# Shared experts in one stage, and expert rows added to the output by an adding scatter DMA

## The chip, the core and the metric

One NeuronCore of a Trainium2 chip runs the whole program in one launch. The metric is the device time of a run in microseconds, the median of several runs. The engines are PE (TensorE), DVE (VectorE), ACT (ScalarE), POOL (GpSimd) and SP (SyncE, which here only issues DMAs). They run side by side and are ordered by semaphores alone.

## The reference

Sixteen sequences of 512 tokens, width 256, all float32. A layer-normed attention block with 16 heads comes first, then a mixture-of-experts block. What matters here is the second half:

```python
x = x + attention(layernorm(x))                # called x1 below
xf = layernorm(x)                              # 8192 rows of 256
w  = top-2 of softmax(layernorm(xf) @ gate_w.T), normalised
out = swiglu(xf, sWg, sWu, sWd)                # the shared expert, every row
for e in range(8):                             # 256 -> 512 -> 256 each
    out = out + w[:, e:e+1] * swiglu(xf, Wg[e], Wu[e], Wd[e])
x = x + out
```

## The kernel before, in words

The attention stage and a short route stage come first and are not touched but for one table. The route stage gives each token two places in a list `xs_d` of 135 slots of 128 rows, sorted by expert; a slot belongs to one expert. `place` holds, for each token and choice, the row where the result goes and its weight. Then come three stages, each a block that all engines leave together.

**Scatter stage** (`scatter_stage`). ACT writes each tile of 128 normed rows into a ring buffer (L1460, L1462), and POOL scatters it twice into `xs_d` with an indirect DMA (L1491): 64 tiles, 128 scatters. Beside this the stage runs the shared expert (`SharedExpert`) for the first 11 of the 16 sequences. Its work is cut in rounds, one per sequence: PE does gate and up products (L1067) in four parts, the transposes of the next sequence (L1054), and after the second part the down products of the sequence before (L1081); ACT does the silu (L1116) and after each of the four parts writes some tiles' rows, `A_ROUND = (1, 2, 1, 2)` of them; DVE adds x1 to the result (`ysb`, L1183), and SP stores it to `ys_d`. All rounds are unrolled and each engine's order is written out by hand.

**Expert stage** (`expert_stage`). A loop over the 135 slots, software-pipelined over three slots. POOL loads a slot's rows (`xr`, L1594) two slots ahead and, two slots behind, scatters the slot's weighted result `y_e` (L1733) with an indirect DMA to `y2_d` (L1599). The destination `to` is the row in `y2_d` that belongs to the token and its choice; unused rows of a slot go to a spare row of their own. On each slot POOL issues the load first and then waits for `y_e`:

```python
pool.dma_start(xr[:, s.par], rows_of(xs_v, s.plus(2)))...
d = s.plus(-2)
pool.wait_ge(y_taken, d.v + 1)
nc.gpsimd.indirect_dma_start(y2_d[:, :], ...to[:, d.quad]..., y[:, d.par], None)
    .then_inc(y_stored[d.par], 16)
```

**Combine stage** (`combine_stage`). It loads the shared expert's weights again, runs the shared expert for the last five sequences, and adds the two expert results of each token to the shared result: on POOL for the first 11 sequences, on DVE for its own five. It reads `ys_d` and `y2_d` and writes the output.

Of the kernel before, what the change touches and what calls it, by code (L numbers as in the profile page):

```python
# [30 lines left out]
P = 128  # L31
# [22 lines left out]
SHARED_FIRST = 11  # L54
# [80 lines left out]
def build(nc, x, wqT, bq, wkT, bk, wvT, bv, woT, bo, J, lam, lns, lnb, gwT, Wg, Wu, Wd, sWg, sWu, sWd, out):  # L135
# [6 lines left out]
    ys_d = nc.dram_tensor("ys_d", [NT, P, D], F32, kind="Internal").ap()  # L142
    xs_d = nc.dram_tensor("xs_d", [NSLOT * P, XW], F32, kind="Internal").ap()
    y2_d = nc.dram_tensor("y2_d", [(NSLOT + 2 * NT) * P, D], F32, kind="Internal").ap()

    top = ExitStack()
    with top:
# [16 lines left out]
        with ExitStack() as c:  # L164
            moe_stages(nc, c, sbt, gws, gwb, lgT, Wg, Wu, Wd, sWg, sWu, sWd, out,
                       x1_d, ys_d, xs_d, y2_d, whi_d, wlo_d, ident, ones, mv2, eps)
# [756 lines left out]
def moe_stages(nc, ctx, sbt, gws, gwb, lgT, Wg, Wu, Wd, sWg, sWu, sWd, out,  # L923
               x1_d, ys_d, xs_d, y2_d, whi_d, wlo_d, ident, ones, mv2, eps):
    pos = sbt(ctx, "pos", [P, NT, 2], I32)
    slot_e = sbt(ctx, "slot_e", [1, NSLOT], I32)
    rstd2 = sbt(ctx, "rstd2", [P, NT])
    nmr = sbt(ctx, "nmr", [P, NT])
    place = sbt(ctx, "place", [P, NT, 2, 2])
    shared_weights = (sWg, sWu, sWd)  # L930

    with ExitStack() as c:
        with nc.cleanup_on_exit(), ExitStack() as c1:
            route_stage(nc, c1, sbt, ident, ones, mv2, eps, rstd2, nmr, place, lgT, gws, gwb, pos, slot_e)
        with ExitStack() as c1:
            scatter_stage(nc, c1, sbt, shared_weights, x1_d, ys_d, xs_d, ident, mv2, rstd2, nmr, place, pos)
    with ExitStack() as c:
        expert_stage(nc, c, sbt, whi_d, wlo_d, xs_d, y2_d, ident, slot_e)
    with ExitStack() as c:
        combine_stage(nc, c, sbt, shared_weights, x1_d, y2_d, ys_d, out, ident, mv2, rstd2)  # L940


class SharedExpert:
# [3 lines left out]
    def __init__(self, nc, ctx, sbt, tag, base, count, weights, x1_d, ys_d, ident, mv2, rstd2):  # L947
# [7 lines left out]
        self.x1_d, self.ys_d, self.ident, self.mv2, self.rstd2 = x1_d, ys_d, ident, mv2, rstd2  # L955
# [35 lines left out]
        self.a_store = 32 if base == 0 else 16  # L991
# [31 lines left out]
    def store(self, eng, s):  # L1023
        if not self.has(s):
            return
        ys_v = self.ys_d.rearrange("(c t) p d -> c p t d", t=TT)
        for j in range(2):
            eng.wait_ge(self.y_taken, s.v * 2 + j + 1)
            eng.nop(nofuse=True)
            eng.dma_start(self.batch_of(ys_v, s)[:, 2 * j:2 * j + 2], self.ysb[:, s.par, j]).then_inc(self.y_stored[s.par], 16)  # L1030
# [145 lines left out]
    def outputs(self, dve, s):  # L1176
        dve.wait_ge(self.x1_loaded[s.par], (s.half() + 1) * 16)
        for j in range(2):
            dve.wait_ge(self.y_ready, s.v * 2 + j + 1)
            if s.at_least(2) and j == 0:  # L1180
                dve.wait_ge(self.y_stored[s.par], s.half() * self.a_store)
# [18 lines left out]
def route_stage(nc, ctx, sbt, ident, ones, mv2, eps, rstd2, nmr, place, lgT, gws, gwb, pos, slot_e):  # L1200
# [76 lines left out]
    def _(pool):  # L1277
# [7 lines left out]
        nc.gpsimd.iota(place[:, :, :, 0].rearrange("p (b t) r -> p b t r", t=TT), pattern=[[S, NB], [1, TT], [NT * P, 2]], base=NSLOT * P,  # L1285
                       channel_multiplier=TT, allow_small_or_imprecise_dtypes=True).then_inc(iotas, 1)
# [100 lines left out]
def scatter_stage(nc, ctx, sbt, shared_weights, x1_d, ys_d, xs_d, ident, mv2, rstd2, nmr, place, pos):  # L1387

    FIRST, RING, AHEAD = SHARED_FIRST, 8, 3
    A_ROUND = (1, 2, 1, 2)  # L1390
# [6 lines left out]
    se = SharedExpert(nc, ctx, sbt, "_1", 0, FIRST, shared_weights, x1_d, ys_d, ident, mv2, rstd2)  # L1397
# [99 lines left out]
def expert_stage(nc, ctx, sbt, whi_d, wlo_d, xs_d, y2_d, ident, slot_e):  # L1497
# [15 lines left out]
    spare = sb("spare", [P, NSLOT])  # L1513
# [19 lines left out]
    spare_ready = sem("spare_ready")  # L1533
# [19 lines left out]
    xs_v = xs_d.rearrange("(s p) d -> s p d", p=P)  # L1553
    def over_slots(eng, step):
# [24 lines left out]
    def _(pool):  # L1579
        for r in range(2):  # L1580
            pool.dma_start(xr[:, r], xs_v[r]).then_inc(x_loaded[r], 16)
        nc.gpsimd.iota(spare[:], pattern=[[P, NSLOT]], base=0, channel_multiplier=1,
                       allow_small_or_imprecise_dtypes=True).then_inc(spare_ready, 1)

        def step(s):
# [9 lines left out]
            if exists(s.plus(-2)):  # L1595
# [3 lines left out]
                nc.gpsimd.indirect_dma_start(y2_d[:, :], bass.IndirectOffsetOnAxis(ap=to[:, d.quad], axis=0), y[:, d.par], None)\  # L1599
# [111 lines left out]
    def _(dve):  # L1711
# [33 lines left out]
        def destination(s):  # L1745
# [7 lines left out]
        dve.wait_ge(spare_ready, 1)  # L1753
# [3 lines left out]


def combine_stage(nc, ctx, sbt, shared_weights, x1_d, y2_d, ys_d, out, ident, mv2, rstd2):


    def sem(name):
        return ctx.enter_context(nc.semaphore(name))

    BASE, OWN = SHARED_FIRST, NB - SHARED_FIRST
    RING = 3
    acc = sbt(ctx, "acc", [P, RING, TT, D])
    yr = sbt(ctx, "yr", [P, RING, 2, TT, D])
    yo = sbt(ctx, "yo", [P, 2, 2, TT, D])
    loaded = [sem(f"loaded{r}") for r in range(RING)]  # L1770
    stored = [sem(f"stored{r}") for r in range(RING)]
    own_loaded = [sem(f"own_loaded{r}") for r in range(2)]
    final_done = sem("final_done")
    own_done = sem("own_done")
    se = SharedExpert(nc, ctx, sbt, "_2", BASE, OWN, shared_weights, x1_d, ys_d, ident, mv2, rstd2)
    block = ctx.enter_context(nc.Block())
    ys_v = ys_d.rearrange("(b t) p d -> b p t d", t=TT)
    y2_v = y2_d[NSLOT * P:, :].rearrange("(r b p t) d -> b p r t d", r=2, b=NB, p=P)
    out_v = out.rearrange("b (t p) d -> b p t d", p=P)

    @block.sync
    def _(sp):
        def load_rows(b):

            r = b % RING
            if b >= RING:
                sp.wait_ge(final_done, (b - RING + 1) * 2)
            sp.dma_start(yr[:, r], y2_v[b]).then_inc(loaded[r], 16)
            if b >= RING:
                sp.wait_ge(stored[r], b // RING * 16)  # L1790
            sp.dma_start(acc[:, r], ys_v[b]).then_inc(loaded[r], 16)

        def store(b):

            sp.wait_ge(final_done, (b + 1) * 2)
            sp.dma_start(out_v[b], acc[:, b % RING]).then_inc(stored[b % RING], 16)

        def load_own(o):

            if o >= 2:  # L1800
                sp.wait_ge(own_done, (o - 1) * 2)
            sp.dma_start(yo[:, o % 2], y2_v[BASE + o]).then_inc(own_loaded[o % 2], 16)

        def store_own(o):

            sp.wait_ge(own_done, (o + 1) * 2)
            sp.dma_start(out_v[BASE + o], se.ysb[:, o % 2].rearrange("p j t d -> p (j t) d")).then_inc(se.y_stored[o % 2], 16)

        se.load_in(sp, Batch(0, 0))
        se.load_weights(sp)  # L1810
        se.load_in(sp, Batch(0, 1))
        se.load(sp, Batch(0, 0))
        load_rows(0)
        se.load(sp, Batch(0, 1))
        se.load_in(sp, Batch(0, 2))
        load_rows(1)
        load_own(0)
        for b in range(2, RING):
            load_rows(b)
        load_own(1)  # L1820

        held = 0
        for s in range(OWN + 1):
            if s >= 1:
                se.load_in(sp, Batch(0, s + 2))
            for _ in range(2 if s < OWN else BASE - held):
                store(held)
                if held + RING < BASE:
                    load_rows(held + RING)
                held += 1  # L1830
            if s >= 1:
                store_own(s - 1)
                se.load(sp, Batch(0, s + 1))
                if s + 1 < OWN:
                    load_own(s + 1)
        for r in range(RING):
            sp.wait_ge(stored[r], (BASE - r + RING - 1) // RING * 16)
        for r in range(2):
            sp.wait_ge(se.y_stored[r], (OWN + 1 - r) // 2 * 16)

    @block.gpsimd
    def _(pool):
        for b in range(BASE):
            r = b % RING
            pool.wait_ge(loaded[r], (b // RING + 1) * 32)
            nc.gpsimd.tensor_tensor(acc[:, r], acc[:, r], yr[:, r, 0], ALU.add).then_inc(final_done, 1)
            pool.wait_ge(final_done, b * 2 + 1)
            nc.gpsimd.tensor_tensor(acc[:, r], acc[:, r], yr[:, r, 1], ALU.add).then_inc(final_done, 1)

    @block.tensor  # L1850
    def _(pe):
        se.transposes(pe, Batch(0, 0))
        pe.wait_ge(se.w_lo, 3)
        for s in range(OWN + 1):
            se.tensor_round(pe, Batch(0, s))

    @block.scalar
    def _(act):
        se.split_weights_hi(act)
        se.copies(act, Batch(0, 0))  # L1860
        for s in range(OWN + 1):
            se.scalar_round(act, Batch(0, s), lambda s, i: None)

    @block.vector
    def _(dve):
        def own_final(o):

            dve.wait_ge(own_loaded[o % 2], (o // 2 + 1) * 16)
            dve.wait_ge(se.y_taken, o * 2 + 2)
# [44 lines left out]
```

## Time and profile before

| | us |
|---|---|
| median of 3 runs (lowest to highest) | 2273.76 (2270.4 to 2279.28) |
| the profiled execution | 2278.09 |
| its span, first to last instruction | 2276.5 |
| scatter stage (1224.2 to 1478.4 of the span) | 254.2 |
| expert stage (1478.4 to 2151.4) | 673.0 |
| combine stage (2151.4 to 2276.5) | 125.1 |

The profile gives, for one execution, each instruction's start and length, what ended the idle time of its engine before it (the releaser), and the DMA traffic. The profiled execution's own time is 1.6 us more than its span and 4.3 us above the median of the runs. An arrow `<-` between tiles reads "written from"; after a wait it names the releaser; "issue" is a wait for nothing that the profile shows, and "remote" one whose releaser it could not name. The trace calls `y2_d` `y_d`. PE's ends are modelled.

### The profile page before, as it was taken

Reading aid. Unit: us, or ns where it says so; the run is one execution under the profiler, and the core shown is the slowest. Engines: PE = TensorE matmul, PEld = TensorE weight load, DVE = VectorE, ACT = ScalarE, POOL = GpSimd, SP = SyncE. Lnnn points to the kernel's source line nnn. Section 1 sums busy time; section 2 is a strip of 40 time slices with the busy share of each in tenths; the row PEclk is TensorE's granted clock in tenths of the full one; section 3 lists DMA queues with packets and bytes.
Section 4 is the critical chain, followed back from the end, with each engine's and each line's share of the span. In section 5 each row is a group of like instructions: output and inputs, shape, how many; then the busy total and the mean of one; then the engine's idle time right before and its main releaser. Section 6 shows DMA issues by size and latency. Waiting matters only on the chain. (4 is left out here: it accounts for less than half of the span.)

```text
span 2276.5 us, 47620 instructions
## 1 busy us (share of the span) xinstructions
PE 1993.5 (88%) x14698; PEld 1308.5 (57%) x14767; DVE 1289.2 (57%) x3898; ACT 1085.5 (48%) x2357; POOL 757.6 (33%) x1173
## 2 busy tenths in 40 slices
PE   2789999999999999999863988789999999999687
PEld 1344444545444454444432877667777777777576
DVE  5556666776666677666636443334554544455376
ACT  1155555555555555555422444345555555555331
POOL 1033333333333333333310555423333333333263
PEclk8599999999999999999975999989999999999899
DMA  7033344434334443433213555473111111111297
GB/s 211 29 112 110 114 132 133 123 117 126 110 114 132 133 125 115 126 110 105 89 63 111 179 185 178 145 297 133 56 56 57 57 57 55 57 55 57 101 330 270
DMA packets 156032, 276.87 MB, mean 122 GB/s; under 512 B 28576, under 2 KB 85152, under 8 KB 154848
## 3 DMA queue, kind: packets, MB, share of 16 engines
q1 hardware_dynamic: 133312, 219.13, 29.9%
q0 software_dynamic: 19104, 54.35, 7.1%
q8 instruction: 91, 1.49, 0.3%
q10 hardware_dynamic: 3456, 1.34, 0.2%
q14 instruction: 69, 0.57, 0.1%
HBM read 136.01 MB, written 96.26 MB: 102 GB/s over the span
## 5 line engine op out<-in xcount | busy, mean ns | idle before, releaser
L633 DVE CUSTOM_DVE_ANT_0 ps_rows<-ps_rows,maskrow 128x512 f32<-128x512 f32 (+3 forms) x1024 | 484.5, 515 | 304.3 <-PE ps_rows L490 303.4
L578 ACT ACTIVATE probs<-ps_cols 128x512 f32<-128x512 f32 (+3 forms) x1024 | 392.1, 435 | 387.7 <-PE ps_cols L501 381.1
L490 PE MATMUL ps_rows<-ks,qs 32*128 32x512 f32 (+3 forms) x2048 | 427.2, 492 | 85.7 <-DVE mx L633 48.7
L497 PE MATMUL ps_cols<-qs,ks 32*128 32x512 f32 (+3 forms) x2048 | 418.7, 485 | 2.5 <-ACT probs L578 2.4
L490 PEld LDWEIGHTS ps_rows<-ks,qs 32*128 32x128 f32 x2048 | 161.6, 188 | 294.9 <-DVE mx L633 245.6
L752 POOL TENSOR_TENSOR pace<-eps 1x1 f32<-1x1 f32 x256 | 58.4, 228 | 777.8 <-ACT probs L578 777.8
L501 PE MATMUL ps_cols<-mT,ones_r 32*128 32x512 f32 (+3 forms) x1024 | 285.3, 550 | 0.0
L1599 POOL DMA_INDIRECT y_d<-y_e,to x135 | 136.4, 1010 | 335.1 <-DVE y_e L1733 321.2
L1725 DVE TENSOR_TENSOR h_lo<-ps_h,h_hi 128x512 fp32r<-128x512 f32 x135 | 93.4, 692 | 229.5 <-ACT h_hi L1700 229.5
L1694 ACT ACTIVATE sg_e<-ps_ge 128x512 f32<-128x512 f32 x135 | 80.9, 599 | 264.2 <-PE ps_ge L1620 264.2
L514 PE MATMUL ps_o<-probs,vt 128*32 128x512 f32 (+3 forms) x2048 | 192.7, 448 | 0.8 <-POOL probs L754 0.8
L1491 POOL DMA_INDIRECT xs_d<-row,pos x128 | 128.5, 1004 | 155.4 <-ACT row L1462 123.4
L754 POOL TENSOR_SCALAR_AFFINE_SELECT probs<-probs 128x512 f32<-128x512 f32 x256 | 160.6, 627 | 0.0
L497 PEld LDWEIGHTS ps_cols<-qs,ks 32*128 32x128 f32 x2048 | 154.5, 184 | 9.3 <-ACT probs L578 7.6
L633 DVE DVE_READ_ACCUMULATOR2_ANT mx<- 128x1 f32 x1024 | 145.0, 142 | 0.1
L1067 PE MATMUL ps_g<-x2T,swg 128*128 128x512 f32 x384 | 107.2, 416 | 31.8 <-ACT sg L1116 15.4
L1741 DVE TENSOR_TENSOR h_e<-sg_e,ps_ue 128x512 f32<-128x512 f32 x135 | 92.9, 688 | 72.5 <-PE ps_ue L1620 72.5
L501 PEld LDWEIGHTS ps_cols<-mT,ones_r 32*128 32x128 f32 x1024 | 99.4, 188 | 51.5 <-issue 31.9
L1594 POOL DMA_DIRECT2D xr<-xs_d x133 | 73.7, 554 | 120.0 <-DVE to L1751 111.3
L1081 PE MATMUL ps_y<-swd,hT 128*128 128x256 f32 x768 | 100.8, 292 | 11.8 <-DVE hT L1164 8.3
L1620 PE MATMUL ps_ge<-w_hi,x_lo 128*128 x270 | 110.9, 492 | 0.0
L1620 PE MATMUL ps_ue<-w_hi,x_lo 128*128 x270 | 110.4, 490 | 0.0
(212 smaller groups left out, 3847.3 us busy)
## 6 DMA issues: line engine op xcount, KB each, us to landing
xs_d<-zrows SPq DMA_DIRECT2D x45, 408.0 KB, 2.9
xr<-xs_d POOLq DMA_DIRECT2D x135, 136.0 KB
whi_d<-w_sh SPq DMA_DIRECT2D x16, 768.0 KB, 3.8
w_hi<-whi_d SPq DMA_DIRECT2D x8, 1536.0 KB
yr<-y_d SPq DMA_DIRECT2D x11, 1024.0 KB, 8.0
xn<-in_L_attn_x_dram SPq DMA_DIRECT2D x16, 512.0 KB, 5.0
ks<-k_lin SPq DMA_DIRECT2D x64, 128.0 KB, 3.1
ks<-k_tan SPq DMA_DIRECT2D x64, 128.0 KB, 3.7
```

The costliest lines, as they stand in the source:

```text
L490: mm = nc.tensor.matmul(ps_rows[bank_of(row_no(g, it, h))][:, 0:(it + 1) * P], qs[at:at + STRIP, d.par, g, it * P:(it + 1) * P], ks[at:at ...
L497: nc.tensor.matmul(ps_cols[bank_of(col_no(n, s, e))][:, jt * P:S], ks[at:at + STRIP, b.par, gc, jt * P:(jt + 1) * P], qs[at:at + STRIP, b. ...
L501: mm = nc.tensor.matmul(ps_cols[bank_of(col_no(n, s, e))][:, jt * P:S], ones_r[at:at + STRIP], mT[at:at + STRIP, gc % 2, jt * P:S], start= ...
L514: mm = nc.tensor.matmul(ps_o[2 * HD * h:2 * HD * (h + 1), jt * P:S], vt[:, b.par, jt, g * HG + h], probs[:, n % 2, h, jt * P:S], start=jt ...
L578: nc.scalar.activation(probs[:, n % 2, 2 * (1 - s) + e, jt * P:S], ps_cols[bank_of(col_no(n, s, e))][:, jt * P:S], ACT.Exp).then_inc(exp_d ...
L633: nc.vector.tensor_tensor_reduce(out=bank, in0=bank, in1=maskrow[:, (TT - 1 - it) * P:S], scale=1.0, scalar=LOWEST, op0=ALU.add, op1=ALU.m ...
L754: nc.gpsimd.affine_select(out=blk, in_=blk, compare_op=ALU.is_ge, fill=0.0, base=0, pattern=[[0, HG], [1, P]], channel_multiplier=-1).then ...
L1067: mm = nc.tensor.matmul(bank[i % 2][:], w[:, wp, k, i * P:(i + 1) * P], self.x2T[:, s.par, xp, k], start=at == 0 and k == 0, stop=at == 2 ...
L1081: mm = nc.tensor.matmul(self.ps_y[j][:, tt], self.hT[:, s.par, hp, i, t * P:(t + 1) * P], self.wd[:, wp, i], start=at == 0 and i == 0, sto ...
L1491: nc.gpsimd.indirect_dma_start(xs_d[:, :], bass.IndirectOffsetOnAxis(ap=pos[:, t, r:r + 1], axis=0), row[q][:, r], None).then_inc(scattere ...
L1599: nc.gpsimd.indirect_dma_start(y2_d[:, :], bass.IndirectOffsetOnAxis(ap=to[:, d.quad], axis=0), y[:, d.par], None)\
L1620: mm = nc.tensor.matmul(bank, part[:, k], w[side][:, k * width:(k + 1) * width], start=at == 0 and k == 0, stop=at == 2 and k == n - 1)
```

## The change

The shared expert runs for all 16 sequences in the scatter stage and stores straight into the output; ACT's tiles per round become `(1, 1, 1, 2)`. The expert stage scatters `y_e` with an adding indirect DMA into the output itself. Each adding scatter waits for the one before it to have landed, since two slots can hold rows of the same token. Unused rows get a destination out of bounds and are skipped by a bounds check. The combine stage, `ys_d`, `y2_d` and `spare` are gone.

```diff
-SHARED_FIRST = 11
+BEYOND = 1 << 14
...
-        nc.gpsimd.iota(place[:, :, :, 0].rearrange("p (b t) r -> p b t r", t=TT), pattern=[[S, NB], [1, TT], [NT * P, 2]], base=NSLOT * P,
-                       channel_multiplier=TT, allow_small_or_imprecise_dtypes=True).then_inc(iotas, 1)
+        nc.gpsimd.iota(place[:, :, :, 0], pattern=[[P, NT], [0, 2]], base=-BEYOND, channel_multiplier=1,
+                       allow_small_or_imprecise_dtypes=True).then_inc(iotas, 1)
...
-        ys_v = self.ys_d.rearrange("(c t) p d -> c p t d", t=TT)
+        out_v = self.out.rearrange("b (t p) d -> b p t d", p=P)
...
-    FIRST, RING, AHEAD = SHARED_FIRST, 8, 3
-    A_ROUND = (1, 2, 1, 2)
+    FIRST, RING, AHEAD = NB, 8, 3
+    A_ROUND = (1, 1, 1, 2)
...
                 d = s.plus(-2)
                 pool.wait_ge(y_taken, d.v + 1)
                 pool.nop(nofuse=True)
-                nc.gpsimd.indirect_dma_start(y2_d[:, :], bass.IndirectOffsetOnAxis(ap=to[:, d.quad], axis=0), y[:, d.par], None)\
+                if d.at_least(1):
+                    before = d.plus(-1)
+                    pool.wait_ge(y_stored[before.par], (before.half() + 1) * 16)
+                    pool.nop(nofuse=True)
+                nc.gpsimd.indirect_dma_start(out_v, bass.IndirectOffsetOnAxis(ap=to[:, d.quad], axis=0), y[:, d.par], None,
+                                             bounds_check=NT * P - 1, oob_is_err=False, compute_op=ALU.add)\
                     .then_inc(y_stored[d.par], 16)
...
-            own = spare[:, s.off:s.off + 1] if s.fixed else spare[:, bass.ds(s.v, 1)]
             nc.vector.tensor_copy(share[:, s.quad], xr[:, s.par, D + 1:D + 2]).then_inc(share_ready, 1)
-            nc.vector.tensor_tensor(to[:, s.quad], xr[:, s.par, D:D + 1], own, ALU.max).then_inc(to_ready, 1)
+            nc.vector.tensor_scalar(to[:, s.quad], xr[:, s.par, D:D + 1], float(BEYOND), None, ALU.add).then_inc(to_ready, 1)
...
-def combine_stage(nc, ctx, sbt, shared_weights, x1_d, y2_d, ys_d, out, ident, mv2, rstd2):
```

## Rows read from the trace of the kernel before

**Rows 1.** The page: the span, and busy tenths in 40 equal slices.
```profile
span 2276.5 us, 47620 instructions
...
PE   2789999999999999999863988789999999999687
...
DMA  7033344434334443433213555473111111111297
```

**Rows 2.** Windows: start:end length, PE PEld DVE ACT POOL, clock, DMA, GB/s.
```profile
1224.20:1478.40 254.20, 213.66 (x1144) 181.67 (x1144) 103.40 (x187) 114.56 (x242) 128.54 (x128) 0.91 0.51 178
...
1478.40:2151.40 673.00, 648.04 (x3982) 496.56 (x4050) 324.17 (x810) 340.11 (x675) 211.49 (x271) 0.99 0.24 82
...
2151.40:2276.50 125.10, 95.45 (x520) 82.71 (x520) 79.92 (x93) 30.73 (x53) 55.42 (x22) 0.88 0.84 302
...
1540.00:2130.00 590.00, 584.41 (x3609) 449.11 (x3670) 294.18 (x737) 308.24 (x612) 191.98 (x245) 1.00 0.19 62
```

**Rows 3.** The chain that ended last: start, length, what. The combine stage.
```profile
2152.75 7.57 DMA sw_in<-in_L_ffn_sWd_dram
...
2208.49 5.75 PE ps_y L1081 x48
...
2226.03 5.75 PE ps_y L1081 x48
```

**Rows 4.** Timeline of the scatter stage, PE: three of the down products.
```profile
1258.84 2.87 PE L1081 MATMUL ps_y<-swd,hT 128*128 128x256 f32 x20
...
1453.66 5.92 PE L1081 MATMUL ps_y<-swd,hT 128*128 128x256 f32 x48
...
1469.05 6.00 PE L1081 MATMUL ps_y<-swd,hT 128*128 128x256 f32 x48 [2.17 <-DVE hT L1164]
```

**Rows 5.** Timeline of the scatter stage: one burst of scatters, and who waited.
```profile
1404.63 0.96 POOL L1491 DMA_INDIRECT xs_d<-row,pos  x1 [4.17 <-ACT row L1462]
...
1416.97 1.55 PE L1067 MATMUL ps_g<-x2T,swg 128*128 128x512 f32 x6
...
1419.38 0.96 POOL L1491 DMA_INDIRECT xs_d<-row,pos  x1 [0.30 <-issue]
...
1422.29 0.60 ACT L1116 ACTIVATE sg<-ps_g 128x512 f32<-128x512 f32 x1 [8.63 <-PE ps_g L1067]
...
1424.48 0.96 POOL L1491 DMA_INDIRECT xs_d<-row,pos  x1 [4.14 <-ACT row L1462]
```

**Rows 6.** Wait in the scatter stage: us in total, times, longest.
```profile
ACT sg L1116 <- remote: 63.7, 8, 9.1
```

**Rows 7.** Timeline of the expert stage: steady part, one slot, the stage's end.
```profile
1541.13 1.01 POOL L1599 DMA_INDIRECT y_d<-y_e,to  x1 [2.43 <-DVE y_e L1733]
...
1801.10 0.48 DVE L1733 TENSOR_SCALAR y_e<-ps_ye,share 128x256 f32<-128x256 f32 x1 [0.22 <-PE ps_ye L1620]
...
1802.36 1.01 POOL L1599 DMA_INDIRECT y_d<-y_e,to  x1 [2.53 <-DVE y_e L1733]
...
1804.09 0.55 POOL L1594 DMA_DIRECT2D xr<-xs_d  x1 [0.72 <-DVE to L1751]
...
2128.89 1.01 POOL L1599 DMA_INDIRECT y_d<-y_e,to  x1 [2.56 <-DVE y_e L1733]
...
2144.46 0.96 POOL L1599 DMA_INDIRECT y_d<-y_e,to  x1 [0.81 <-DVE y_e L1733]
...
2151.40 0.32 SPq L1021 DMA_DIRECT2D xin<-x_d  x1
```

**Rows 8.** DMA busy tenths in 40 slices of 0.12 us from 1802.3.
```profile
DMA  0000000000000679500000000998431000000000
```

**Rows 9.** DMA busy tenths in 40 slices of 0.075 us from 1475.5.
```profile
DMA  0000000000000000289899998962000000000000
```

**Rows 10.** Waits of SP's queue at the end of the scatter stage.
```profile
SPq L935 <- DMA ys_d<-ysb: 1.7, 1, 1.7
```

**Rows 11.** Wait in the expert stage: us in total, times, longest.
```profile
POOL y_d L1599 <- DVE y_e L1733: 309.5, 126, 2.7
```

More of the change, by code:

```diff
@@ L141, in build @@
     x1_d = nc.dram_tensor("x1_d", [NB, P, TT, D], F32, kind="Internal").ap()
-    ys_d = nc.dram_tensor("ys_d", [NT, P, D], F32, kind="Internal").ap()
     xs_d = nc.dram_tensor("xs_d", [NSLOT * P, XW], F32, kind="Internal").ap()
-    y2_d = nc.dram_tensor("y2_d", [(NSLOT + 2 * NT) * P, D], F32, kind="Internal").ap()
     top = ExitStack()
@@ L165, in build @@
             moe_stages(nc, c, sbt, gws, gwb, lgT, Wg, Wu, Wd, sWg, sWu, sWd, out,
-                       x1_d, ys_d, xs_d, y2_d, whi_d, wlo_d, ident, ones, mv2, eps)
+                       x1_d, xs_d, whi_d, wlo_d, ident, ones, mv2, eps)
 def attention_stage(nc, ctx, sbt, x_v, wqT, bq, wkT, bk, wvT, bv, woT, bo, J, lam,
@@ L923, in moe_stages @@
 def moe_stages(nc, ctx, sbt, gws, gwb, lgT, Wg, Wu, Wd, sWg, sWu, sWd, out,
-               x1_d, ys_d, xs_d, y2_d, whi_d, wlo_d, ident, ones, mv2, eps):
+               x1_d, xs_d, whi_d, wlo_d, ident, ones, mv2, eps):
     pos = sbt(ctx, "pos", [P, NT, 2], I32)
@@ L935, in moe_stages, with __init__ @@
         with ExitStack() as c1:
-            scatter_stage(nc, c1, sbt, shared_weights, x1_d, ys_d, xs_d, ident, mv2, rstd2, nmr, place, pos)
+            scatter_stage(nc, c1, sbt, shared_weights, x1_d, out, xs_d, ident, mv2, rstd2, nmr, place, pos)
     with ExitStack() as c:
-        expert_stage(nc, c, sbt, whi_d, wlo_d, xs_d, y2_d, ident, slot_e)
-    with ExitStack() as c:
-        combine_stage(nc, c, sbt, shared_weights, x1_d, y2_d, ys_d, out, ident, mv2, rstd2)
+        expert_stage(nc, c, sbt, whi_d, wlo_d, xs_d, out, ident, slot_e)
 class SharedExpert:
-    def __init__(self, nc, ctx, sbt, tag, base, count, weights, x1_d, ys_d, ident, mv2, rstd2):
+    def __init__(self, nc, ctx, sbt, tag, base, count, weights, x1_d, out, ident, mv2, rstd2):
         def sb(name, shape, dt=F32):
@@ L954, in __init__ @@
         self.nc, self.base, self.count, self.weights = nc, base, count, weights
-        self.x1_d, self.ys_d, self.ident, self.mv2, self.rstd2 = x1_d, ys_d, ident, mv2, rstd2
+        self.x1_d, self.out, self.ident, self.mv2, self.rstd2 = x1_d, out, ident, mv2, rstd2
         self.w_in = sb("sw_in", [P, 3, KT * INTER])
@@ L1029, in store @@
             eng.nop(nofuse=True)
-            eng.dma_start(self.batch_of(ys_v, s)[:, 2 * j:2 * j + 2], self.ysb[:, s.par, j]).then_inc(self.y_stored[s.par], 16)
+            eng.dma_start(self.batch_of(out_v, s)[:, 2 * j:2 * j + 2], self.ysb[:, s.par, j]).then_inc(self.y_stored[s.par], 16)
     def split_weights_hi(self, act):
@@ L1180, in outputs @@
             if s.at_least(2) and j == 0:
-                dve.wait_ge(self.y_stored[s.par], s.half() * self.a_store)
+                dve.wait_ge(self.y_stored[s.par], s.half() * 32)
             self.nc.vector.tensor_tensor(self.ysb[:, s.par, j], self.ps_y[j][:], self.x1[:, s.par, 2 * j:2 * j + 2], ALU.add)\
@@ L1384, in _, with scatter_stage @@
         then(nc.vector.tensor_scalar(slot_e[:], cnt[:], float(NE - 1), None, ALU.min))
-def scatter_stage(nc, ctx, sbt, shared_weights, x1_d, ys_d, xs_d, ident, mv2, rstd2, nmr, place, pos):
-    FIRST, RING, AHEAD = SHARED_FIRST, 8, 3
-    A_ROUND = (1, 2, 1, 2)
+def scatter_stage(nc, ctx, sbt, shared_weights, x1_d, out, xs_d, ident, mv2, rstd2, nmr, place, pos):
+    FIRST, RING, AHEAD = NB, 8, 3
+    A_ROUND = (1, 1, 1, 2)
     row = [sbt(ctx, f"row{q}", [P, 2, XW]) for q in range(RING)]
@@ L1396, in scatter_stage @@
     scattered = [ctx.enter_context(nc.semaphore(f"scattered{q}")) for q in range(RING)]
-    se = SharedExpert(nc, ctx, sbt, "_1", 0, FIRST, shared_weights, x1_d, ys_d, ident, mv2, rstd2)
+    se = SharedExpert(nc, ctx, sbt, "_1", 0, FIRST, shared_weights, x1_d, out, ident, mv2, rstd2)
     block = ctx.enter_context(nc.Block())
@@ L1494, in _, with expert_stage @@
             pool.wait_ge(scattered[q], (NT - q + RING - 1) // RING * 32)
-def expert_stage(nc, ctx, sbt, whi_d, wlo_d, xs_d, y2_d, ident, slot_e):
+def expert_stage(nc, ctx, sbt, whi_d, wlo_d, xs_d, out, ident, slot_e):
     def sb(name, shape, dt=F32):
@@ L1553, in expert_stage @@
     xs_v = xs_d.rearrange("(s p) d -> s p d", p=P)
+    out_v = out.rearrange("b s d -> (b s) d")
     def over_slots(eng, step):
@@ L1581, in _ @@
             pool.dma_start(xr[:, r], xs_v[r]).then_inc(x_loaded[r], 16)
-        nc.gpsimd.iota(spare[:], pattern=[[P, NSLOT]], base=0, channel_multiplier=1,
-                       allow_small_or_imprecise_dtypes=True).then_inc(spare_ready, 1)
         def step(s):
@@ L1756, in _ @@
         over_slots(dve, step)
-def combine_stage(nc, ctx, sbt, shared_weights, x1_d, y2_d, ys_d, out, ident, mv2, rstd2):
[L1762 to L1869, printed above, removed]
-            y = se.ysb[:, o % 2].rearrange("p j t d -> p (j t) d")
-            nc.vector.tensor_tensor(y, y, yo[:, o % 2, 0], ALU.add).then_inc(own_done, 1)
-            dve.wait_ge(own_done, o * 2 + 1)
-            nc.vector.tensor_tensor(y, y, yo[:, o % 2, 1], ALU.add).then_inc(own_done, 1)
-        se.norm(dve, Batch(0, 0))
-        se.split_weights_lo(dve)
-        se.lower_rows(dve, Batch(0, 0))
-        se.norm(dve, Batch(0, 1))
-        for s in range(OWN + 1):
-            for i in range(IT):
-                se.vector_unit(dve, Batch(0, s), i)
-                if i == 2 and s >= 1:
-                    own_final(s - 1)
-            if se.has(Batch(0, s)):
-                se.lower(dve, Batch(0, s), IT - 1)
```

4 lines of the change are left out of this document (removed).

## The prediction

> **What bounds the kernel now.** I read the page first, for the three stages that the change touches: PE is nearly full while the DMA queues swing between idle and full, so the question in each stage is who makes PE wait [rows 1]. The windows by stage then give 254.2, 673.0 and 125.1 us [rows 2].
>
> The expert stage is PE's: from 1540 to 2130 PE is busy 584.4 of 590.0 us at clock 1.00, with a DMA share of only 0.19 [rows 2]. The timeline gives its pace: the 9th of the 135 result scatters starts at 1541.13 and the 131st at 2128.89, so 587.76 / 122 = 4.82 us a slot [rows 7].
>
> The combine stage is in two parts. Weight load, splitting and the first sequences take from 2151.4 to 2208.5; then a round lasts 2226.03 − 2208.49 = 17.5 us, the PE work of one sequence back to back [rows 3].
>
> The scatter stage is slower at the same PE work. Its down products start at 1258.84 and, nine rounds on, at 1453.66: 21.65 us a round, 4.1 above the 17.5 [rows 4]. The timeline shows why. POOL issues twelve scatters in a burst (1404.63 the first, 1419.38 the last, 1.27 apart with the gaps), the burst's last ends at 1420.34, and only at 1422.29 does ACT begin a silu whose product PE had started at 1416.97 and ended at 1418.5; POOL then idles 4.14 us until ACT's next row [rows 5]. Such late releases add up to 63.7 us on ACT alone, with no releaser named [rows 6]. So a round here is a burst plus a fixed remainder: 12 × 1.27 = 15.2, and 21.65 − 15.2 = 6.4 us.
>
> **What goes: the combine stage.** All 125.1 us [rows 2]. Nothing of it stays for the end: the expert stage's last scatter starts at 2144.46 and the next stage's first instruction at 2151.40 [rows 7]; that wait for the landing and for POOL to leave the block lies inside the expert stage's 673.0 and will now be the kernel's end. The reads of the results and of `ys_d` and the final adds go with it.
>
> **What moves: five sequences into the scatter stage.** Head and tail of the stage stay (34.6 us ahead of the first down product, 15.4 from the last-but-one to the last, 9.3 behind it [rows 4]). Between them 9 rounds become 14. With five tiles a round the 64 tiles last 13 rounds, so some 11.5 of the 14 carry a burst of ten scatters, 12.7 us. By the remainder above such a round is 12.7 + 6.4 = 19.1 us, still above 17.5; the other 2.5 run at PE's pace. That is 219.7 + 44 = 264, against 194.8 now: **+69 us**. The bounds: every round at PE's pace, 14 × 17.5 − 194.8 = +50; the burst rounds as slow as today, 11.5 × 21.65 + 44 − 194.8 = +98. I take the middle because the release follows the burst's end by the row. Per moved sequence SP's queue also gets two loads of 512 KB and two stores of 256 KB, and the stores change their target and not their shape; this is 1.5 MB in some 18 us, in a stage whose DMA share is 0.51 [rows 2]. POOL gets nothing more: still 128 scatters. The iota for `place` and the stores to the output cost what they did.
>
> **What is added: the adding scatter and its wait.** This decides the sign. Today a scatter starts at 1802.36, its data move from about 1803.9 to 1804.5 [rows 8], and the landing follows the data closely: at the stage's end before, a 256 KB store moved its data until about 1477.5 [rows 9] and SP's wait on it, 1.7 us long, ended at 1477.9 [rows 10]. So a plain scatter lands some 0.4 us after its data, 2.5 us after its start. Nobody waits for that now: POOL waits for `y_e` (309.5 us in 126 waits) [rows 11].
>
> After the change POOL's next scatter needs the landing of the last one. From `y_e`'s end at 1801.58 to the scatter's start are 0.78 us [rows 7], which I take for the way from any release to a start. The wait hides as long as landing + 0.78 ≤ 4.82, so up to a landing of 4.04 us. The extra room is 1.5 us. Queued behind the waiting scatter on POOL is the next `xr` load (1804.09, data until 1806.1 [rows 7, 8]), and behind that PE's transposes; DVE waits too, before it overwrites `y_e` and `to`. If the landing is late, the whole loop takes the pace landing + 0.78.
>
> No row shows an adding DMA. Lower bound: nothing extra, 2.5 us. An added read of the same 128 rows: the `xr` load's data take 0.8 us against 0.6 for the scatter [rows 8], so a read run ahead of the write gives about 3.3 us. Above that: a whole load (1804.09 to 1806.1 plus 0.4, so 2.4 us) before a whole scatter, 4.9 us. The far end: the eight rows that each of the 16 DMA engines has of a scatter strictly one behind another, each row paying 0.4 us of landing for its read and as much for its write beside 0.15 of transfer: 1.5 + 8 × 0.95 = 9.1 us. I take 3.3: in both cases the DMA engines stream their rows without gaps, and the added work is one more stream of the same size at a DMA share of 0.19. So in the steady part nothing is added; the work that hides it is PE's 4.8 us a slot, and without that cover every microsecond would cost 131 us.
>
> The Trainium skill bears on this in "DMA: Bandwidth & Descriptors", section Two DMAs through the same engine are not ordered: a second read-modify-write packet of a row read stale data when it directly followed the first, and none did once five packets separated them. That says such packets overlap, which by itself would strike out the gross rival below and leave the sum as it is; no run here shows it.
>
> Before 1540 the expert weights still load; some eight slots run with busy DMA engines there [rows 1], and their landings can be late by up to 0.9 us each beyond the room (the 4.9 case): I take +5, bounds 0 and 7. The last landing is about 1 us later. The bounds check and the one DVE instruction that replaces another for `to` lie off the path: POOL's two instructions take 1.56 of 4.82 us a slot [rows 7].
>
> **Sum.** −125.1 + 69 + 5 + 1 = −50 us. The span goes to 2226, the profiled execution to 2228, and the median of 2273.76 to **2224**. With the scatter bounds the hidden case reaches from 2273.8 − 125.1 + 50 + 1 = 2200 to 2273.8 − 125.1 + 98 + 8 = 2255.
>
> **The rivals.**
> *The wait takes over, mildly.* The read stands ahead of the write as a whole, landing 4.9 us: pace 5.7, so (5.68 − 4.82) × 131 = +113, to **2337**. The landing from which it decides is 4.04 + 50/131 = 4.4 us. For it: 1.5 us is little room for a round trip to HBM. Against: the streams in the rows overlap. The skill has a rule on its side, "DMA: Bandwidth & Descriptors", Latency and other measured facts: HBM access takes 0.2 us on average and 2 us under high load; as an estimate, a landing of 2.7 or of 4.5, the first hidden, the second some 60 us dear; the DMA share in this stage speaks for the first.
> *The wait takes over, grossly.* Rows go one by one in each DMA engine: landing 9.1, pace 9.9, +664 us, to **2890**; at half that cost a row, landing 5.3, it is +165, to 2390. For it: an adding packet may not stream as a copying one. Against: only that no row shows such a stop between packets.
> *The scatter stage gives no round back.* Rounds with bursts stay at 21.65: +98 in place of +69, to **2253**. For it: nothing names what holds PE's signals, and it may depend on the round and not on the burst. The other way, rounds at PE's pace, gives **2205**.
>
> **How the numbers follow.** Hidden wait 0.62, of it 0.12 for the slow scatter rounds and 0.1 for the fast; landing of 4.1 to 4.5, within 11 us of no change or a little faster, 0.05; 4.5 to 5.3 us 0.17; above that 0.16. A measurement of this kernel can tell about 0.5%, 11 us, from no change. So faster 0.64, same 0.03, slower 0.33. The likeliest case alone spans 2200 to 2255; the range for 8 in 10 has to reach over the mild case, to 2390, and leaves out the gross one and a little below.
>
> **What would show it.** Right: no stage behind the expert stage; expert slots still 4.8 us apart; POOL's adding scatter waiting for `y_e` and not for its own last DMA; scatter-stage rounds of about 19 us for the first 12 and 17.5 after, the stage near 323 us. Wrong: POOL waiting on the DMA of the line before, with the slot pace equal to that landing plus 0.8, PE idle and its clock falling; or scatter rounds of 21 us or more.

## The result, and the profile after

The changed kernel takes 2224.7 us in the median of 4 runs (2222.39 to 2224.97), the kernel before beside it 2276.5 (2270.4 to 2293.1). The ratio is 0.9754, 95% interval 0.9716 to 0.9791: faster. The profiled execution has a span of 2220.7 us, 55.8 less than before. Its stages, by windows (start:end length, busy time of PE, PEld, DVE, ACT, POOL, then clock, DMA share, GB/s):

```profile
1227.00:1529.10 302.10, 284.41 (x1664) 251.82 (x1664) 148.57 (x267) 141.80 (x292) 131.24 (x128) 0.97 0.51 176
1529.10:2220.70 691.60, 652.18 (x3982) 499.75 (x4050) 322.66 (x810) 339.93 (x675) 297.33 (x270) 0.98 0.37 79
...
1558.50:1609.00 50.50, 36.48 (x198) 26.57 (x200) 14.47 (x38) 16.91 (x33) 13.25 (x13) 0.90 0.78 264
1609.00:2200.00 591.00, 586.34 (x3630) 452.43 (x3692) 294.54 (x739) 309.74 (x615) 272.83 (x247) 1.00 0.33 56
```

Against [rows 2] that is 302.1 for 254.2 in the scatter stage (+47.9), 691.6 for 673.0 in the expert stage (+18.6), −125.1 for the combine stage, and a start of the scatter stage at 1227.0 and not 1224.2 (+2.8; in the profiled runs of this study that start lies anywhere between 1217.6 and 1229.6, in code that does not differ). The sum is −55.8.

**Scatter stage.** The down products on PE's timeline, which answer to [rows 4]:

```profile
1261.28 6.00 PE L1076 MATMUL ps_y<-swd,hT 128*128 128x256 f32 x48
...
1278.82 6.00 PE L1076 MATMUL ps_y<-swd,hT 128*128 128x256 f32 x48
...
1489.38 6.00 PE L1076 MATMUL ps_y<-swd,hT 128*128 128x256 f32 x48
...
1519.68 6.00 PE L1076 MATMUL ps_y<-swd,hT 128*128 128x256 f32 x48 [2.17 <-DVE hT L1159]
```

From 1261.28 to 1489.38 are 13 rounds of 17.55 us: every round runs at PE's pace, though most of them carry a burst of ten scatters. The signals of PE's finished products still come late on this chip, but it costs nothing. One burst, answering to [rows 5]:

```profile
1407.52 0.96 POOL L1486 DMA_INDIRECT xs_d<-row,pos  x1 [0.30 <-issue]
...
1410.07 0.69 DVE L1178 TENSOR_TENSOR ysb<-ps_y,x1s 128x512 f32<-128x512 f32 x1 [2.25 <-remote]
1410.15 0.60 ACT L1111 ACTIVATE sg<-ps_g 128x512 f32<-128x512 f32 x1 [6.78 <-PE ps_g L1062]
...
1412.34 0.96 POOL L1486 DMA_INDIRECT xs_d<-row,pos  x1 [3.85 <-ACT row L1457]
```

The last scatter of the burst ends at 1408.48. ACT's silu comes at 1410.15, some 1.7 us behind it and 1.1 us after PE had ended its product (started at 1407.48). In the kernel before it came 3.8 us after the product's end [rows 5]. With two scatters fewer a round, the burst ends before PE runs out of work that needs no signal.

The rounds before were not alike. Seen from one down product to the next they took 18.3 to 24.4 us, since the twelve scatters of a round often fell apart into ten and two. The silu came 1.9 to 2.1 us behind nearly every burst of ten or twelve. So what differs between the kernels is the scatters in a round, not whether one burst has ten or twelve.

**Expert stage.** The adding scatter as the trace groups it, with its landing, and the page's row for it:

```profile
L1596 POOL DMA_INDIRECT out_dram<-y_e,to x135: 1542/1595/1666, 1552.5 to 2213.8; - x135
...
  DMA out_dram<-y_e,to: 193.6, 76
  DVE to L1748: 78.1, 27
...
DMA to landing us min/median/max: 2.7/3.8/8.6
```
```profile
L1596 POOL DMA_INDIRECT out_dram<-y_e,to x135 | 215.5, 1596 | 369.6 <-DMA out_dram<-y_e,to 193.6
```

It lands 3.8 us after its start in the median, 8.6 at most, and POOL's instruction for it lasts 1.6 us and not 1.01. POOL now waits for its own last scatter 76 times. Of these, 74 lie behind 1609, where the wait is 2.6 us at most: the landing comes last there by a little, but within PE's pace. In the timeline the waits sort themselves by what else is moving:

```profile
1558.51 1.59 POOL L1596 DMA_INDIRECT out_dram<-y_e,to  x1 [3.62 <-DVE to L1748]
...
1567.08 1.59 POOL L1596 DMA_INDIRECT out_dram<-y_e,to  x1 [6.38 <-PE ps_x L1628]
...
1576.45 1.60 POOL L1596 DMA_INDIRECT out_dram<-y_e,to  x1 [7.18 <-PE ps_x L1628]
...
1585.90 1.59 POOL L1596 DMA_INDIRECT out_dram<-y_e,to  x1 [7.24 <-DMA out_dram<-y_e,to]
...
1595.08 1.60 POOL L1596 DMA_INDIRECT out_dram<-y_e,to  x1 [6.98 <-DVE to L1748]
...
1604.31 1.59 POOL L1596 DMA_INDIRECT out_dram<-y_e,to  x1 [7.00 <-PE ps_x L1628]
...
1608.97 1.60 POOL L1596 DMA_INDIRECT out_dram<-y_e,to  x1 [2.47 <-DVE to L1748]
...
1613.63 1.59 POOL L1596 DMA_INDIRECT out_dram<-y_e,to  x1 [2.44 <-DMA out_dram<-y_e,to]
```

Five gaps in a row, from 1558.51 to 1604.31, are 8.6 to 9.5 us; from there on they are 4.7. The first group lies beside SP's loads of the expert weights (DMA share 0.78 from 1558.5 to 1609, 0.33 after). The releaser that the rows name changes, and often it is an instruction that had ended earlier. The chain that ended last names the landing:

```profile
1567.08 8.52 DMA out_dram<-y_e,to
1576.45 8.61 DMA out_dram<-y_e,to
1585.90 8.32 DMA out_dram<-y_e,to
...
1785.62 1.40 PE ps_ye L1618 x12
1795.22 1.40 PE ps_ye L1618 x12
```

8.52 us of landing and a gap of 9.37, 8.61 and 9.45, 8.32 and 9.18: a slot takes the landing plus 0.85. From then on the chain is PE's down products every 9.60 us, two slots. The steady part has no cost: PE is busy 586.3 of 591.0 us. Counted from the stage's start, the ninth scatter begins after 84.5 us (1613.63 − 1529.10) and not after 62.7 (1541.13 − 1478.40), so 21.8 us are lost on the first nine slots, and the rest of the stage is 3.2 us shorter than before.

### The profile page after: what moved, and what is told of

Same layout as the page of the kernel before. It is cut to its first block and busy times, and to the rows that moved or that the text cites. A ratio compares the mean times of both kernels' runs of the same rounds, so it can differ in the third digit from the quotient of the medians.

```text
span 2220.7 us, 47761 instructions
## 1 busy us (share of the span) xinstructions
PE 1972.8 (89%) x14698; PEld 1300.3 (59%) x14767; DVE 1252.4 (56%) x3885; ACT 1081.6 (49%) x2354; POOL 789.4 (36%) x1150
## 5 line engine op out<-in xcount | busy, mean ns | idle before, releaser
L1596 POOL DMA_INDIRECT out_dram<-y_e,to x135 | 215.5, 1596 | 369.6 <-DMA out_dram<-y_e,to 193.6
L1587 POOL DMA_DIRECT2D xr<-xs_d x133 | 117.5, 883 | 18.8 <-DVE to L1748 17.6
L1062 PE MATMUL ps_g<-x2T,swg 128*128 128x512 f32 x384 | 99.3, 394 | 6.7 <-DVE x2T L1168 6.7
L1062 PE MATMUL ps_u<-x2T,swu 128*128 128x512 f32 x384 | 98.4, 392 | 0.0
```

Source lines behind the costliest of these rows:

```text
L1062: mm = nc.tensor.matmul(bank[i % 2][:], w[:, wp, k, i * P:(i + 1) * P], self.x2T[:, s.par, xp, k], start=at == 0 and k == 0, stop=at == 2 ...
L1587: pool.dma_start(xr[:, s.par], rows_of(xs_v, s.plus(2))).then_inc(x_loaded[s.par], 16)
L1596: nc.gpsimd.indirect_dma_start(out_v, bass.IndirectOffsetOnAxis(ap=to[:, d.quad], axis=0), y[:, d.par], None, bounds_check=NT * P - 1, oob ...
```

## The experiments

The kernel before varied between the chips: 2276 to 2281 us in the median on those of all runs but the fifth to the eighth, 2249 on theirs. A ratio is always taken on one chip.

**1. Six tiles a round again.**

```diff
-    A_ROUND = (1, 1, 1, 2)
+    A_ROUND = (1, 2, 1, 2)
```

> The changed kernel with six tiles a round again, (1, 2, 1, 2) in place of (1, 1, 1, 2); nothing else differs. Theory A (the number of scatters in a burst sets when PE's signals come through, and with it the round): the first 10 or 11 rounds go back to about 21.6 us and the stage grows by some 10 x 4.1 = 40 us, from 302 to about 340; the time is about 2263 where before is 2275. Theory B (the faster rounds come from something else, such as the stores to the output): rounds stay at 17.5 us and the time at about 2225.

Measured: 2258.8 us, ratio 0.9888 (0.9837 to 0.9940). The next stage's first load starts at 1562.1 and this one's at 1225.9, so the scatter stage takes 336 us; ACT's waits with no releaser named are back at 61.7 us (63.7 in [rows 6]). The number of tiles in a round decides, not the stores or the 16 sequences. By the medians some 34 us of the 52 come from this one line (2258.8 − 2224.7, two chips; runs 10 and 11 give 33 on one, with the pair of tiles in another place).

**2. A plain scatter, with the wait.**

```diff
-    bounds_check=NT * P - 1, oob_is_err=False, compute_op=ALU.add)\
+    bounds_check=NT * P - 1, oob_is_err=False)\
```

> The changed kernel with a plain copying scatter in place of the adding one, with the same wait and bounds check; it leaves out the adding, so that the rows hold only the last expert's result. Theory A (the add's late landing, while expert weights load, is what made the expert stage 18.6 us longer): landing back to about 2.5 us (5 to 6 beside the weight load), POOL no longer waits on its own DMA in the steady part, expert stage about 675 to 680 us, in all about 2210. Theory B (the wait and the bounds check cost it by themselves): the stage stays at 690. The length of POOL's scatter instruction, 1.6 us against 1.0 before, shows whether add or bounds check lengthens it.

Measured: 2210.0 us, ratio 0.9685 (0.9640 to 0.9731); expert stage from 1528.9 to 2207.8, 678.9 us.

```profile
L1596 POOL DMA_INDIRECT out_dram<-y_e,to x135: 983/1022/1037, 1552.1 to 2201.2; - x135
...
DMA to landing us min/median/max: 2.1/2.4/7.1
```

The instruction is back at 1.02 us, so the add lengthens it and not the bounds check; the landing is 2.4 us, and 7.1 at most. With the wait in place the add costs 12.7 us of stage; all else that changed in the stage costs 5.9. Windows of one slot show what the add does to the packets, here the plain scatter and a row load:

```profile
DMA packets 96, 0.27 MB, mean 56 GB/s; under 512 B 32, under 2 KB 32, under 8 KB 96
```

and here the same two transfers in the changed kernel:

```profile
DMA  0000000000000000009859799969888010000000
...
DMA packets 192, 0.27 MB, mean 56 GB/s; under 512 B 32, under 2 KB 160, under 8 KB 192
```

The counts are cumulative, and the bytes are the same. Between 512 B and 2 KB lie 128 packets (160 − 32) in place of none, one for each row of 1 KB. From 2 KB up there are 32 in place of 64: the copy takes four rows to a packet, as the row load does in both. The adding scatter's data move from about 1805.2, 2.2 us after its start at 1803.0, and run on into the row load.

**3. The add without POOL's wait.**

```diff
-                if d.at_least(1):
-                    before = d.plus(-1)
-                    pool.wait_ge(y_stored[before.par], (before.half() + 1) * 16)
-                    pool.nop(nofuse=True)
```

> The changed kernel without POOL's wait for the scatter before; DVE's wait for the scatter two slots before, ahead of writing y_e, stays, so at most two adding scatters are in flight. Two scatters side by side hold rows of two slots that stand next to each other, which share no token with these inputs. Theory A (the wait on a late landing beside the weight load costs the 18.6 us): a landing of 8.5 us shared by two gives a pace under 5 us, expert stage about 675, in all about 2208. Theory B (the add's traffic on the DMA engines costs it, by late row loads or late weights): the stage stays near 690. In the steady part theory A and B both expect 4.80 us a slot.

Measured: 2207.1 us, ratio 0.9679 (0.9630 to 0.9728); expert stage from 1526.1 to 2202.6, 676.5 us. Theory A holds: with the add in place and the wait gone the stage is 15 us shorter. Runs 2 and 3 each take away one of the two and gain 13 and 15 of the 18.6 us, so the cost belongs to the add and the wait together. POOL waits for `y_e` again:

```profile
POOL out_dram L1592 <- DVE y_e L1727: 298.7, 119, 3.3
```

This version rests on the data: it may have the scatters of two neighbouring slots in flight, and would lose an addition if an expert had so few tokens that they shared one.

**4. Weight loads paced.**

```diff
         for e in range(NE):
+            if e >= 2:
+                sp.wait_ge(tx_ready, 10 * (e - 1))
+                sp.nop(nofuse=True)
```

> The changed kernel with SP's loads of the expert weights from the third expert on held back until slots 10, 20, ... 60 have been turned, so that each meets two or three adding scatters and is not part of one long stretch. Theory A (each adding scatter that lands beside a weight load costs about 4.5 us, five to six of them today): a load of 2.3 MB delays one or two landings by less than the 8.5 us seen, so six loads cost 6 x 2 to 6 x 5 us; between 10 us less and 10 us more than now, expert stage 682 to 702. Rival: only the uninterrupted stretch hurts and single loads hide, stage about 675.

Measured: 2219.2 us, ratio 0.9725 (0.9679 to 0.9770); expert stage from 1530.1 to 2216.8, 686.7 us. Five us less than the changed kernel, inside what theory A gave; the rival's 675 is not met, so a single load of 2.3 MB does not hide either: behind the load that starts at 1580.73, one pair of scatters is 8.5 us apart (1582.09 to 1590.62).

**5. The kernel before with its pair moved.**

```diff
-    A_ROUND = (1, 2, 1, 2)
+    A_ROUND = (2, 1, 1, 2)
```

> The kernel before with its six tiles a round placed (2, 1, 1, 2) in place of (1, 2, 1, 2): the same count, the pair moved from behind the second part of a round to behind the first. Theory A (the number of tiles in a round decides): rounds stay at about 21.6 us, the time at 2275 or so. Theory C (what decides is the pair behind the second part, whose scatters then run beside the down products): rounds fall toward 17.5 us and the time by up to 9 x 4.1 = 37 us, to about 2240.

Measured: 2245.1 us, but the kernel before beside it 2249.3; ratio 0.9997 (0.9966 to 1.0027). The profiled execution has its rounds at 17.55 us, and its scatter stage takes 215.3 us in place of 254.2:

```profile
1251.38 6.00 PE L1081 MATMUL ps_y<-swd,hT 128*128 128x256 f32 x48
...
1391.75 6.00 PE L1081 MATMUL ps_y<-swd,hT 128*128 128x256 f32 x48
```

Read alone this would have spoken for theory C. It does not, since the unchanged kernel was as fast there. No profile of the latter was taken on this chip, so that its rounds were fast there is not shown, only that its time was 27 us lower than elsewhere. Run 5's combine stage took 135.7 us and not 125.1, which takes part of the gain back; why is not known.

**6. The changed kernel with its pair moved.**

```diff
-    A_ROUND = (1, 1, 1, 2)
+    A_ROUND = (1, 2, 1, 1)
```

> The changed kernel with its five tiles a round placed (1, 2, 1, 1) in place of (1, 1, 1, 2): the same count, the pair moved behind the second part. Theory A (count): rounds stay at 17.5 us, the time at about 2225. Theory C (place): rounds go up toward 21 us, the time by up to 12 x 3.5 = 42 us, to about 2265.

Measured: 2222.6 us, ratio 0.9868 (0.9820 to 0.9917) against the 2249.3 us of the kernel before on that chip; rounds at 17.55 us. After run 5 this tells nothing about place. It tells two other things. The change, with its pair moved, was worth 26.6 us here, where the same kernel in run 11 gained 53.6 on its chip. And the signals of PE were on time on this chip even with five tiles. One silu in run 6, and the same one in run 11, which is the same kernel on another chip:

```profile
1408.88 1.55 PE L1062 MATMUL ps_g<-x2T,swg 128*128 128x512 f32 x6
...
1410.46 0.60 ACT L1111 ACTIVATE sg<-ps_g 128x512 f32<-128x512 f32 x1 [4.90 <-PE ps_g L1062]
```
```profile
1409.55 1.55 PE L1062 MATMUL ps_g<-x2T,swg 128*128 128x512 f32 x6
...
1412.27 0.60 ACT L1111 ACTIVATE sg<-ps_g 128x512 f32<-128x512 f32 x1 [6.03 <-PE ps_g L1062]
```

In run 6 the silu starts as its product ends (1408.88 + 1.55 = 1410.43), 0.6 us after the burst; in run 11 it starts 1.2 us after its product and 1.7 us after the burst.

**7. Half the scatters.**

```diff
-    A_ROUND = (1, 1, 1, 2)
+    A_ROUND = (1, 2, 1, 2)
...
-            for r in range(2):
+            for r in range(1):
                 nc.gpsimd.indirect_dma_start(xs_d[:, :], ...
```

> The changed kernel with (1, 2, 1, 2) again, and one scatter a tile in place of two; it leaves out the second choice's rows, so only the scatter stage is read. ACT writes as many rows as in the run with six tiles, POOL issues half the scatters. Theory A or C (POOL's scatters hold PE's signals): rounds at 17.5 us, stage about 302. Rival (ACT's row writing holds the round): rounds stay above 20 us, stage about 336.

Measured, in one run: 2224.4 us, rounds at 17.55 us, stage 302.4 us. As expected by theory A, but on the same chip, where run 5's six tiles were not slow either: it excludes nothing. So whether POOL's scatters or ACT's row writing hold a slow round was not told apart by an experiment; for POOL speaks that the silus follow the bursts' ends.

**8. One more load behind each adding scatter.**

```diff
...
+                pool.dma_start(extra[:, d.par], whi_d[0][:, 0].rearrange("p k n -> p (k n)")).then_inc(extra_in[d.par], 16)
...
```

> The changed kernel with one more load of 512 KB on POOL's queue right behind each adding scatter, into a buffer that nobody reads. It adds 1.3 to 1.5 us of DMA traffic a slot, in a stage whose DMA share is 0.33. Theory A (a slot takes the larger of PE's 4.80 us and the add's landing plus 0.78): the landing goes from 3.8 to about 5, a slot to 5.8 us, the stage up by about 120 us. Rival (a share of 0.33 leaves room enough): landing under 4, slots at 4.80.

Measured, in one run: 2240.4 us. Theory A's number fell, and the rival's came.

```profile
DMA  6666666666676767667666766666667666766666
...
extra<-whi_d POOLq DMA_DIRECT2D x122, 512.0 KB, 5.3
...
out_dram<-y_e,to POOLq DMA_INDIRECT x123, 3.9
```
```profile
1610.00:2200.00 590.00, 586.85 (x3643) 446.89 (x3643) 291.15 (x733) 305.50 (x607) 342.13 (x367) 1.00 0.68 164
```

The DMA share is 0.68 in place of 0.33, yet the add lands after 3.9 us and PE is busy 586.9 of 590.0 us. The 16 us more lie outside this window, in the part where the weights load and at the end. So the mean amount of traffic does not make the add late. The extra load stands behind the add on the same queue; the expert weights come from SP's queue, beside it. The extra load is also over when the next add's data start: for the scatter of 1803.44 the DMA engines are idle from 1804.9 to 1805.6 ahead of them. Queue and moment are thus not told apart by this run.

**9 to 11. Both counts of tiles on a chip with slow rounds.** First the kernel before, unchanged, for its profile:

> The kernel before, unchanged, for a profile on the chip that the next three runs use, since its median was 2249 on the chip of the last four runs and 2276 to 2281 elsewhere. Theory D (the late signals of the scatter stage come and go with the chip and the execution, for kernels whose bursts are twelve scatters long): the span differs from 2276.5 in the scatter stage and nowhere else, the rounds' starts showing where. Rival (the difference lies elsewhere): scatter stage 254 us whatever the total.

Measured, in one run: 2276.9 us, span 2275.3, scatter stage 254.8 us, waits with no releaser 62.1 us on ACT: slow rounds as in [rows 4, 6]. Then, on the same chip, the edits of runs 1 and 6 again:

> The changed kernel with (1, 2, 1, 2) once more. Theory A (count of scatters a round) with D: late signals as in the kernel before on the same chip, stage 302 to 340 us, and at least as long as with five tiles. If the rounds are at 17.5 us here while the kernel before has slow ones, theory A falls.

> The changed kernel with (1, 2, 1, 1) once more. Theory A (count): rounds at 17.5 us beside slow ones with six tiles. Theory C (place of the pair): slow rounds as with six tiles. If six tiles show no slow rounds on this chip either, nothing is told apart.

Measured: (1, 2, 1, 2) 2260.4 us, ratio 0.9910 (0.9878 to 0.9942); (1, 2, 1, 1) 2227.8 us, ratio 0.9763 (0.9717 to 0.9809); scatter stages 339.7 and 305.2 us. The first one's down products:

```profile
1281.31 6.00 PE L1076 MATMUL ps_y<-swd,hT 128*128 128x256 f32 x48
...
1469.35 6.00 PE L1076 MATMUL ps_y<-swd,hT 128*128 128x256 f32 x48
...
1486.90 6.00 PE L1076 MATMUL ps_y<-swd,hT 128*128 128x256 f32 x48
...
1504.45 6.00 PE L1076 MATMUL ps_y<-swd,hT 128*128 128x256 f32 x48
```

From 1281.31 to 1469.35 nine rounds of 20.9 us on average, and 17.55 as soon as the tiles are used up. With (1, 2, 1, 1) the rounds are 17.54:

```profile
1280.94 6.00 PE L1076 MATMUL ps_y<-swd,hT 128*128 128x256 f32 x48
...
1298.48 6.00 PE L1076 MATMUL ps_y<-swd,hT 128*128 128x256 f32 x48
...
1491.42 6.00 PE L1076 MATMUL ps_y<-swd,hT 128*128 128x256 f32 x48
```

This pair tells count from place: six tiles slow, five fast, with the pair in the place that theory C blamed. Theory A stands and C falls.

**12. The expert weights in pieces, each behind a landing.**

```diff
+            if e < 2:
...
+            else:
+                for m in range(3):
+                    n = 3 * (e - 2) + m
+                    sp.wait_ge(y_stored[n % 2], (n // 2 + 1) * 16)
+                    sp.nop(nofuse=True)
+                    sp.dma_start(w_hi[:, e, m].bitcast(F32), whi_d[e][:, m].rearrange("p k n -> p (k n)")).then_inc(w_loaded, 16)
+                    sp.dma_start(w_lo[:, e, m], wlo_d[e][:, m].rearrange("p k n -> p (k n)")).then_inc(w_loaded, 16)
...
```

> The changed kernel, its wait kept, with the expert weights from the third expert on loaded in 18 pieces of 768 KB, each started when an adding scatter has landed, one a slot. A piece takes some 2 us and the DMA engines are free for about 2.8 us from a landing to the next scatter's first data. Theory A (only weight traffic on the other queue, side by side with an adding scatter, makes it land at 8.5 us): landings near 3.8 to 4.5 us from the first slot on, expert stage about 677 us, in all about 2208. Rival (pieces still meet the scatters): 18 slots each 1 to 2 us late, stage about 700.

Measured: 2207.1 us in the median of 6 runs (2204.4 to 2208.1), ratio 0.9665 (0.9631 to 0.9700); expert stage 675.5 us, with the wait kept. The landings, beside the pieces and over the whole stage:

```profile
out_dram<-y_e,to POOLq DMA_INDIRECT x18, 4.2
```
```profile
DMA to landing us min/median/max: 2.7/3.8/5.6
```
```profile
1586.52 1.60 POOL L1604 DMA_INDIRECT out_dram<-y_e,to  x1 [2.80 <-DVE to L1756]
...
1591.67 1.59 POOL L1604 DMA_INDIRECT out_dram<-y_e,to  x1 [2.94 <-DMA out_dram<-y_e,to]
...
1597.01 1.60 POOL L1604 DMA_INDIRECT out_dram<-y_e,to  x1 [3.14 <-PE ps_x L1636]
```

Median 4.2 us beside the pieces, 5.6 at most in place of 8.6, slots mostly 4.9 to 5.3 us apart (5.6 and 6.5 once each). This is the best version that does not rest on the data, 17.6 us under the changed kernel by the medians of two chips.

## Why the prediction was right, step by step

The forecast was 2224, inside a range of 2200 to 2390, and faster; 2224.7 was measured. The mechanism that decides the sign was the one forecast: the wait for the landing hides under PE's 4.8 us a slot, and the combine stage's 125.1 us are saved. The slow scatter rounds that the sum counted on did not come, and the cost beside the weight loads was three times the one forecast.

The closeness of the number is luck. In the spans the scatter stage came 21.1 us below its term and the expert stage 12.6 above its two (5 + 1), and the scatter stage began 2.8 later: −55.8 for a forecast of −50. The profiled execution took 2222.4 us and not 2228. The forecast then took the median to lie 4.3 us below the profiled execution, as before; it lay 2.3 above, and that gave the rest back. By the prediction's own figure for rounds at PE's pace, 2205, the number would have been some 20 us low.

Of its signs, two came (no stage behind the expert stage, slots 4.8 us apart) and three did not: the scatter stage was 302.1 us and not near 323, no round took 19 us, and POOL's scatter waited for its own last landing more often than for `y_e` (76 times to 29). In the first slots the sign of being wrong came too: PE idle, with the pace following the landing.

**The combine stage** (−125.1) went whole, and the expert stage's exit wait became the kernel's end, as said: 6.9 us from the last scatter's start to the end of the stage, before and after. The +1 for a later last landing did not show.

**The scatter stage** was put at +69 and came at +47.9, 2 us under the lower bound (+50) that the text kept. The step that was mis-sized is "such a round is 12.7 + 6.4 = 19.1 us". The rule that the release follows the burst's end held (2.0 us before, 1.7 after), though not on the chip of runs 5 to 8. Runs 10 and 11 show that the number of tiles in a round decides. Wrong was to take 6.4 us as a fixed remainder, and every round as one burst of twelve. The 21.65 us were an average over rounds of 18.3 to 24.4 us in which PE had already run dry; ten scatters, 12.7 us, and what follows them fit into 17.55 us. ACT also waited for its input tiles, 14.7 us in run 9 and 2.5 in the changed kernel; whether that is cause or effect of the slow rounds was not taken apart.

**The expert stage's steady part** was forecast as unchanged, for a landing of 3.3 us with room to 4.04. The landing is 3.8 and the stage runs at PE's pace. The base of 2.5 us for a plain scatter was slightly high: the digits of [rows 8] show its data over by 1804.34, which gives 2.4, and run 2 measured 2.4. The stream of reads beside the writes was the right picture, but one term was missing: POOL's instruction is 0.6 us longer with the add (run 2). With it the data start 2.2 us after the scatter's start and not 1.5. The room left is about 0.2 us.

**The part with the weight loads** was put at +5 with a bound of 7. The expert stage's whole surplus is 18.6 us. This is the term that failed: "their landings can be late by up to 0.9 us each beyond the room". They were late by 4.3 to 4.6, with landings up to 8.6. The pace rule itself held with 0.85 in place of 0.78 (8.61 to 9.45, 8.32 to 9.18). Runs 3 and 12 give 15 and 16 us back by taking away the wait or the overlap. Run 8 shows that the mean share of the DMA engines was the wrong measure.

**The rivals.** The wait took over for a handful of slots beside the weight loads and nowhere else, and there with a landing of up to 8.6 us, not the mild rival's 4.9. The gross rival, rows one by one at 0.95 us each, did not come about: all 128 row packets move in about two us, where eight rows an engine at 0.95 us would take 7.6, and land at 3.8. By the rule of the Trainium skill ("DMA: Bandwidth & Descriptors", Two DMAs through the same engine are not ordered) such packets overlap, and the trace agrees as far as it shows that the rows do not wait for one another. By the Trainium skill's figure for HBM access under high load ("DMA: Bandwidth & Descriptors", Latency and other measured facts) the prediction estimated a landing of 4.5 us; beside the weight loads 8.3 to 8.6 were measured, and at a share of 0.68 on one queue 3.9, so mean load alone is not what decides here.

Why 8.6: by the Trainium skill's "DMA: Bandwidth & Descriptors", Queues, rings and completion order, an engine serving two queues takes them in turn, packet by packet. By the counts of run 2 an adding scatter has eight row packets an engine where the copy has two (128 and 32 over 16 engines), and each would wait for a packet of the weights. That agrees with run 2 (a plain scatter suffers less), run 8 (nothing comes between on one queue) and run 12, but no run varied the packets themselves: it is argued, not shown. It also takes each row packet of the profile for one turn, while by the same section of the Trainium skill a turn typically holds 9 to 17 descriptors; no run here shows which it is.

Open stays what makes PE's signals late while POOL issues scatters, and why they were on time in all four profiled executions on the chip of runs 5 to 8, with five tiles and with six.

## What to carry to other kernels

A wait on one's own last DMA was free here as long as landing plus issue path fitted into the pace of the bounding engine, and beyond that cost its full excess on every pass. Its price is to be read in the busiest stretch of DMA traffic from other queues, not in the mean. Where two streams must share the DMA engines, start the bulky one on the landing of the latency-bound one and in pieces that fit the gap: that gave back 16 of 18.6 us. A pacing constant that a change alters in passing can be the larger part of its gain (33 to 34 of 52 us here, on chips with slow rounds): run the change without the constant, before crediting the structure. And a gain from a kernel that sits at such an edge depends on the chip: 26.6 us on one (run 6), 53.6 on another (run 11).

## What the runs showed of the hardware that was not expected

- An adding indirect DMA of 128 rows of 1 KB moved 128 packets, one for each row, against 32 for the copy, with POOL's instruction at 1.60 against 1.02 us and the landing at 3.8 against 2.4 us.
- A load of 512 KB right behind it on the same queue moved its landing by 0.1 us (run 8, one run); weight loads on another queue moved it to 8.3 to 8.6 us.
- The signals of PE's finished products reached ACT mostly 1.6 to 2.1 us after the end of a run of ten or twelve indirect DMAs on POOL, with waits of up to 9 us. Six tiles a round with twelve scatters made slow rounds in the kernel before, in run 1 and in runs 9 and 10. On the chip of runs 5 to 8 run 5 had them at 17.55 us with twelve scatters, and there the signals were on time with five tiles too (run 6).
